# A chunk of the second pass made of every 16th column, and a transposition that reads with a step

## The reference

```python
# layer 0
Ax = adj @ x
h = layernorm(x + 1.0 - 0.1 * x - 0.01 * sum(x * Ax, axis=1))
# layer 1; adj serves as node_adj and as edge_adj, A is adj without its diagonal d
support = concat([(A > 0) @ h, (A < 0) @ h])
edge = gru_cell(support, h, w_ih_e, w_hh_e, b_ih_e, b_hh_e)
hw = h @ W_gat
att = softmax(where(A > 0, e_plus, where(A < 0, e_minus, NEG_INF)), axis=1)
node = gru_cell((att * A) @ hw, h, w_ih_n, w_hh_n, b_ih_n, b_hh_n)
out = layernorm(h + d * edge + d * node)
```

## Time and profile before

| | us |
|---|---|
| median of 3 runs | 1616.17 (1613.36 to 1616.25) |
| the profiled execution, its own time | 1618.01 |
| its span in the profile | 1616.4 |
| first pass, up to about | 700 |
| second pass, 16 blocks, 703 to about | 1582 |
| last small steps | to 1616 |

### The profile page before, as it was taken

One profiled execution on the slowest core, in us unless ns is written; L12 is line 12 of the kernel. 1 busy time (PEld: TensorE's weight loads), 2 busy tenths in 40 slices (PEclk: granted clock), 3 DMA queues, 4 the chain that ended last, 5 costly groups with the idle time before them and its releaser, 6 DMA issues.

```text
span 1616.4 us, 20457 instructions
## 1 busy us (share of the span) xinstructions
PE 1422.6 (88%) x5814; PEld 787.6 (49%) x5814; DVE 1369.9 (85%) x1303; ACT 1204.6 (75%) x1443; POOL 198.3 (12%) x259
## 2 busy tenths in 40 slices
PE   7888888888888888639999999999999999999994
PEld 5555555555555555414444444444444444444442
DVE  6999999999999999758888888888888888889882
ACT  7898888888888888647676677667766776677661
POOL 3000010101010101021111111111111111111100
PEclk9999999999999999959999999999999999999996
DMA  8999999999999999999999999999999999999950
GB/s 272 417 422 422 408 421 408 422 408 422 410 422 410 422 407 422 334 235 345 330 318 312 292 334 306 313 308 327 307 307 293 331 308 303 312 327 304 310 183 8
DMA packets 199358, 548.10 MB, mean 339 GB/s; under 512 B 28832, under 2 KB 34736, under 8 KB 166560
## 3 DMA queue, kind: packets, MB, share of 16 engines
q1 hardware_dynamic: 118112, 405.87, 69.4%
q10 hardware_dynamic: 79872, 138.95, 28.5%
q0 software_dynamic: 1344, 2.99, 0.6%
HBM read 543.56 MB, written 4.19 MB: 339 GB/s over the span
## 4 chain that ended last, share of the span: by engine, by line
PE 44%; DMA 23%; DVE 20%; issue 10%; ACT 2%; DVEq 1%; ACTq 0%; POOL 0%; POOLq 0%; SPq 0%
DMA ring<-in_adj 22%; PE ps L1116 22%; DVE ps L673 14%; PE ps L1128 12%; DVE at L916 2%; PE ps L1164 2%; PE ps L1145 2%; PE ps L1178 2%; PE ps L635 1%; PE ps L1159 1%; PE ps L1169 1%; ACT mask L1035 1%; DMA final<-in_x 1%; ACT final L1046 1%; DVE final L986 0%
## 5 line engine op out<-in xcount | busy, mean ns | idle before, releaser
L1035 ACT ACTIVATE mask<-at 128x2048 fp32r<-128x2048 uint32 x256 | 488.9, 1911 | 260.1 <-DVE at L916 259.8
L916 DVE STREAM_TRANSPOSE at<-ring 128x2048 f32<-128x2048 f32 x256 | 580.1, 2295 | 103.2 <-PE ps L1116 68.7
L635 PE MATMUL ps<-mask,parts 128*128 128x512 f32 x2048 | 542.6, 407 | 117.4 <-DVE ps L673 110.9
L673 DVE SCALAR_TENSOR_TENSOR ps<-ring,ps 128x2048 f32<-128x2048 f32 x256 | 586.4, 2299 | 56.9 <-DMA ring<-in_adj 39.1
L519 ACT ACTIVATE at<-ring 128x2048 bf16<-128x2048 f32 x256 | 488.5, 1909 | 86.2 <-DMA ring<-in_adj 77.5
L1116 PE MATMUL ps<-at,hk 128*64 128x512 f32 x2048 | 472.8, 604 | 45.5 <-DVE at L916 35.3
L635 PEld LDWEIGHTS ps<-mask,parts 128*128 128x128 f32 x2048 | 365.7, 188 | 294.3 <-DVE ps L673 223.0
L1116 PEld LDWEIGHTS ps<-at,hk 128*64 128x64 f32 x2048 | 139.1, 138 | 303.9 <-issue 294.8
L1128 PE MATMUL ps<-mask,parts 128*128 128x512 f32 x1024 | 270.2, 406 | 2.4 <-issue 1.6
L1128 PEld LDWEIGHTS ps<-mask,parts 128*128 128x128 f32 x1024 | 182.2, 188 | 140.4 <-issue 83.3
L785 POOL TENSOR_TENSOR ring<-ring,not_diag 128x256 f32<-128x256 f32 x128 | 94.9, 742 | 746.8 <-DMA ring<-in_adj 729.0
(11 more groups left out here) (155 smaller groups left out, 632.8 us busy)
## 6 DMA issues: line engine op xcount, KB each, us to landing
ring<-in_adj SPq DMA_DIRECT2D x256, 1024.0 KB, 17.7
ring<-in_adj SPq DMA_DIRECT2D x256, 512.0 KB, 9.8
ring<-in_adj ACTq DMA_DIRECT2D x256, 512.0 KB, 10.8
stage<-h_rows POOLq DMA_DIRECT2D x16, 128.0 KB, 7.3
out<-final SPq DMA_DIRECT2D x16, 128.0 KB, 9.5
h_rows<-final ACTq DMA_DIRECT2D x7, 256.0 KB, 9.5
hk<-h_rows ACTq DMA_DIRECT2D x7, 256.0 KB, 24.2
final<-in_x ACTq DMA_DIRECT2D x2, 512.0 KB, 7.6
```

Source lines behind the costliest of these rows:

```text
L635: last = nc.tensor.matmul(ps[:, 4 * (n % 2) + i, :], pair[:, t % 2, e, :], x2[:, cols], start=e == 0, stop=e == 1)
L673: nc.vector.scalar_tensor_tensor(out=gram, in0=ring[:, i % RING, :], scalar=1.0, in1=gram, op0=ALU.mult, op1=ALU.mult, accum_out=flat[:, b ...
L916: nc.vector.transpose(to.rearrange("p c (f q) -> p f c q", q=Q), raw[:, :, 2 * HC * (pair % 2):2 * HC * (pair % 2 + 1), :]).then_inc(s["tu ...
L1035: nc.scalar.activation(pair_view(b["mask"], half // 2)[:, :, cols], pair_view(b["at"], half // 2)[:, :, cols].bitcast(U32), ACT.Sign, accu ...
```

## The change

The 512 columns that a partition group has of a unit were cut into 16 chunks of 32 adjacent columns. Now chunk c has the columns c, c + 16, c + 32 and so on. Three places follow from it.

```diff
@@ rows_back
-    eng.dma_start(b["hk"][Q * g:Q * g + Q, GC * half:GC * (half + 1), :],
-                  h_rows(b, grp).rearrange("(c q) d -> q c d", q=Q)).then_inc(back, 16)
+    eng.dma_start(b["hk"][Q * g:Q * g + Q, GC * half:GC * (half + 1), :].rearrange("q (w c) d -> q w (c d)", c=b["UC"]),
+                  h_rows(b, grp).rearrange("(w q c) d -> q w (c d)", q=Q, c=b["UC"])).then_inc(back, 16)
@@ Fast.vector, turn
-            raw = unit_view(b, v % b["SLOTS"]).rearrange("p (f c q) -> p f c q", f=RH, q=Q)
+            raw = unit_view(b, v % b["SLOTS"]).rearrange("p (f q c) -> p f c q", f=RH, q=Q)
@@ Full.vector, turn
-                "p (f c q) -> p f c q", f=RB, q=Q)
+                "p (f q c) -> p f c q", f=RB, q=Q)
```

## The result

| | before, us | after, us |
|---|---|---|
| median | 1615.67 (1613.36 to 1616.25, 4 runs) | 1850.82 (1850.39 to 1854.39, 4 runs) |
| ratio | | 1.146, 95% interval 1.1447 to 1.1474 |
| span of the profiled execution | 1616.4 | 1852.7 |

A forecast was written before the change was run, and what follows sets the result against it. TensorE bounds the second pass before, VectorE after: a block takes 81.7 us in place of 54.4, 437 us over 16 blocks, so 1616.4 + 437 - 8 = 2045 us. The range is 1780 to 2245 us.

The forecast's parts named there:

- The bound: Second pass: TensorE sets the pace before (53.6 us per block); VectorE becomes the bound after, busy 98% of a block.
- The slack: Second pass: VectorE has 8.2 us idle per block, 0.51 us for each of 16 transpositions, before a slower one decides the time.
- The price of an element read with a step: VectorE's transposition, line 916: 2.14 us more each, about 4.4 us; bounds 0.54 and 1.42 ns more per element.
- doubling: A step doubles the price per element, taken from ScalarE's copies and put on VectorE's transposition: 2.14 us more each.
- part 1: First pass: reads of h in pieces of 4 KB in place of 256 bytes; gain between 0 and 10 us, 8 taken.
- The estimate by the Trainium skill: Whole kernel after the change: 1853 us by its 1.73 ns per column, 2255 us by its 2.50.
- Idle time that goes and stays: VectorE per block: waits of 4.6 us (line 1116) and 2.6 us (line 1068) go, 0.7 + 0.5 = 1.2 us stay.
- the signs that were named: For part 1: windows behind the read of `hk` keep 420 GB/s; first transposition starts up to 8 us before 703.5.
- the eighth read: Read of h issued at 717.87, taking 8.8 us, landed 3.8 us before its first use: faster pieces save nothing there.
- A: Rival: the step is free on VectorE's transposition, leaving only part 1, 1608 us; chance 0.14 with a gain, 0.02 without.
- B: Rival: TensorE loses its clock in second-pass pauses, up to 166 us more, 2211 us; counted within the forecast's 0.80.
- C: Rival: a step of 64 bytes costs VectorE more than any row bounds, above 2243 us, 2590 at 2.09 ns; chance 0.04.

## Why the prediction was right, and what was mis-sized

**The bound.** Right. TensorE had the second pass before, and VectorE has it after, busy 98% of a block. The 98% that the prediction named is the measured share. The range held the time because its two bounds lay 460 us apart; the likeliest value missed by 194 us, on one term.

**The slack.** Right in kind. The run with a step of 3, 0.23 us above the 0.51, costs 92 us, and the run with a step of 2, 0.01 us longer than before, costs nothing. The runs agree with a slack of 0.51 us but don't fix it; the idle time that remains with a step of 3 is twice what the sum kept.

**The price of an element read with a step.** This is the term that was mis-sized. The prediction put 2.14 us more on each transposition, by doubling; measured are 3680 - 2295 = 1385 ns, 0.68 ns per element. 256 x (2.14 - 1.385) = 193 us, and 2045 - 193 = 1852, near the measured time. That it is so near is in part luck. With 1.385 the sum has a block of 46.3 + 22.2 + 1.2 = 69.7 us where 69.1 were measured: VectorE's busy time grew by 21.3 us per block and not by 22.2, which was not traced further, and its idle time is 0.4 us longer than the 1.2. These 9 us too many over 16 blocks are made up for by the 8 us of part 1, of which only about one was there. The doubling came from ScalarE, where 0.78 ns became 1.6, and was carried over as a ratio. The runs show that what carries over between these two engines is the time itself: 1.68 ns per element at a step of 16 on either. The rows held it. ScalarE's 402 ns less a fixed part of 297 - 128 x 0.78 = 197 is 1.60 ns per element; TensorE's weights had given 1.84 ns. Put on VectorE as they are, in place of 1.046, these give 0.55 and 0.79 ns more, 1.13 and 1.62 us per transposition, 1787 and 1914 us in all: bounds around the result, in place of a point above it. The two bounds that the prediction did use, 0.54 and 1.42 ns, held the 0.68.

**The estimate by the Trainium skill.** 1853 us by the 1.73 ns of Vector Engine (DVE) Microarchitecture Reference, section 5.2, against 1850.8 measured. The figure of the Trainium skill is for an instruction with two sources of which one hops 4 KiB, not for a transposition with a step of 64 bytes, and the same two errors of the sum offset each other here; still it lies some 3% above the 1.677 ns measured, and the prediction weighed rows of two other engines above it.

**Idle time that goes and stays.** Right. VectorE's waits on line 1116 and line 1068 are gone in a block; 1.6 us of idle time stay where 1.2 were kept.

**Part 1, pieces of 4 KB.** Too large: 8 us expected, and 1.0 us by the ratio of the run that has it alone, with an interval from a loss of 0.5 to a gain of 2.4. The step that failed is the assignment of both windows' lost transfer time to the pieces. One of them loses 4 to 5% with either size (400 and 405 of 423 GB/s). Of the signs that were named, the second window does keep 420 GB/s and the first does not; the first transposition starts at 700.6, 2.9 us earlier, which a kernel with the small pieces also does. Nothing shows that the eighth read was worth anything, as was said.

**The rivals.** A, a free step, is wrong for 16 floats and would have been right for 2. B is right in its mechanism, the clock falls to 0.92 to 0.94, and wrong in its price, since a TensorE that isn't the bound pays from its pauses. What was held against it, a clock of 1.00 in the first pass at 81 to 85% (rows 9 say 78 to 86%), did not carry over to the longer pauses. C did not occur here but exists: a step of 24 costs 2.50 ns.

## What to carry to other kernels

When a price is brought from one engine to another, ask first whether it is the engine's own or one that both meet in the memory: the price of a stepped read carried over in nanoseconds, not as a ratio. On VectorE, reading floats of SBUF with a step of 2 was free, and every step measured from 4 on cost 0.63 to 0.75 ns more per element, that of 24 1.46 ns; a write was run with a step of 16 alone and cost 0.64. On the engine that bounds the kernel, 16 small weight loads per block with a step of 4 were worth 31 us of 1616. And a transfer that lands three times faster was worth 2.4 us at most here, since hardly anybody waits for its landing.

## What the runs showed of the hardware that was not expected

- An element with a step of 4 or 16 floats costs the same time on VectorE and on ScalarE (1.777 and 1.779 ns, 1.677 and 1.678), though adjacent ones cost 1.042 and 0.833.
- A step of 24 floats costs 2.50 ns per element on VectorE, where 16 costs 1.68 and 4 costs 1.78; by whole instructions less the 138 ns of the fixed part, 32 and 64 cost 1.68 and 6 to 12 cost 1.73 to 1.79. What is special about 24 was not found; no other step that is a multiple of 8 but not of 16, except 8 itself, was run.
- A step of 2 is free on VectorE (2277 against 2274 ns) and not quite on ScalarE (2051 against 1893).
- VectorE's stepped reads are slowed by ScalarE's reads of another tile, and adjacent ones aren't: 3572 ns alone, 3654 beside adjacent and 3682 beside stepped reads of ScalarE, against 2276 to 2278 throughout. ScalarE's stepped copies slow down too, from 3619 to 3745 ns beside stepped transpositions.
- Writing with a step of 16 costs VectorE what reading with it costs (3586 against 3581 ns).
